# Weight casts in pieces of 1024 rows instead of 2048, three of them gated on the layer norm's progress

## The reference

```
xn  = layernorm(x)
s   = causal GQA attention(xn)           # 16 query heads, 4 kv heads, RoPE, then @ Wp.T
Wg  = (gate_w - 128) * gate_scale        # int32 [8192, 2048]; Wu likewise, Wd [2048, 8192]
h   = silu(xn @ Wg.T) * (xn @ Wu.T)
out = x + s * silu(h @ Wd.T)
```

## Time and profile before

| | us |
|---|---|
| median of 2 runs | 5322.83 |
| the two runs | 5040.26 and 5605.40 |
| the profiled execution | 5042.12 |
| its span, first to last instruction, on its slowest core (core 0) | 5039.6 |
| spans of the other seven cores | 4996.3 to 5036.2 |
| TensorE busy | 3874.6 (77% of the span) |
| VectorE, ScalarE, GpSimd busy | 984.7, 699.8, 165.9 |

### The profile page before, as it was taken

The page is one execution under the profiler, slowest core; times in us unless marked ns, Lnnn a source line. Parts: engine busy times, 40 slices in busy tenths (PEclk is TensorE's granted clock), DMA queues, the critical chain, the costliest instruction groups (busy, mean ns, idle before and its releaser), DMA issues.

```text
span 5039.6 us, 50095 instructions; the slowest of 8 cores (4996.3 to 5039.6 us)
## 1 busy us (share of the span) xinstructions
PE 3874.6 (77%) x16768; PEld 1651.2 (33%) x16768; DVE 984.7 (20%) x995; ACT 699.8 (14%) x1076; POOL 165.9 (3%) x308
## 2 busy tenths in 40 slices
PE   0001999939994891999979979999988499948998
PEld 0000444414442340444434432222233144424443
DVE  1111000000000000000024975555511000000010
ACT  0001111101110110111100025555500000000000
POOL 0000000000000000000000000000000000000000
PEclk9999999969997995999989989999999799979999
DMA  9996544785469598544221212100000655564553
GB/s 157 134 145 163 135 118 117 106 135 144 116 110 126 149 115 135 147 116 123 80 55 38 72 42 52 42 14 14 1 25 34 188 111 112 113 199 92 122 114 96
DMA packets 757036, 517.29 MB, mean 103 GB/s; under 512 B 686208, under 2 KB 694416, under 8 KB 743616
## 3 DMA queue, kind: packets, MB, share of 16 engines
q1 hardware_dynamic: 717952, 297.96, 25.8%
q0 software_dynamic: 36544, 207.74, 22.5%
q10 hardware_dynamic: 2304, 8.39, 0.4%
HBM read 329.36 MB, written 197.13 MB: 104 GB/s over the span
## 4 chain that ended last, share of the span: by engine, by line
PE 65%; SPq 17%; DVE 7%; another core or an unknown queue 6%; issue 3%; DMA 2%; ACT 1%; DVEq 0%; POOL 0%; ACTq 0%; POOLq 0%
PE b_ps L57 18%; SPq L57 17%; PE g_ps L57 14%; PE u_ps L57 13%; PE c_ps L57 5%; PE d_ps L57 4%; PE s_ps L57 4%; PE kq_ps L57 4%; PE o_ps L57 3%; DVE rc L57 1%; DVE tmpB L57 1%; DVE tmpA L57 1%; DVE qst L57 1%; DVE lc L57 1%
## 5 line engine op out<-in xcount | busy, mean ns | idle before, releaser
L57 PE MATMUL g_ps<-xnT,gu 128*128 128x512 bf16 x4096 | 901.6, 381 | 540.2 <-DMA gu<-wg_s 477.6
L57 PE MATMUL u_ps<-xnT,gu 128*128 128x512 bf16 x4096 | 903.7, 382 | 247.7 <-DVE h L57 241.4
L57 PE MATMUL b_ps<-wdr,hT 128*128 128x512 bf16 x4096 | 903.1, 384 | 193.5 <-DMA wdr<-wd_s 144.2
L57 PEld LDWEIGHTS g_ps<-xnT,gu 128*128 128x128 bf16 x4096 | 402.2, 98 | 1029.3 <-issue 551.1
L57 PEld LDWEIGHTS u_ps<-xnT,gu 128*128 128x128 bf16 x4096 | 402.7, 98 | 739.0 <-issue 261.7
L57 PEld LDWEIGHTS b_ps<-wdr,hT 128*128 128x128 bf16 x4096 | 404.5, 99 | 692.1 <-issue 220.8
L57 DVE SCALAR_TENSOR_TENSOR h<-u_ps,us_col,sil 128x2048 bf16<-128x2048 f32 x64 | 150.4, 2351 | 2022.3 <-PE u_ps L57 1560.1
L57 ACT ACTIVATE E<-s_ps 128x512 bf16<-128x512 f32 (+3 forms) x576 | 303.1, 526 | 209.5 <-PE s_ps L57 192.2
L57 ACT ACTIVATE sil<-g_ps,gs_col 128x2048 bf16<-128x2048 f32 x64 | 125.9, 1966 | 1393.8 <-PE g_ps L57 1393.7
L57 PE MATMUL kq_ps<-xnT,wsl 128*128 128x512 bf16 x1280 | 281.4, 381 | 32.5 <-DMA wsl<-wk_s 28.6
L57 PE MATMUL d_ps<-E,ones_bf 128*128 128x512 bf16 x640 | 253.8, 397 | 55.1 <-DVE E L57 48.6
(11 more groups left out here) (48 smaller groups left out, 1026.4 us busy)
## 6 DMA issues: line engine op xcount, KB each, us to landing
dwi<-dw SPq DMA_DIRECT2D x64, 1024.0 KB, 5.8
wg_s<-gw POOLq DMA_DIRECT2D x4, 8192.0 KB, 94.4
wu_s<-uw POOLq DMA_DIRECT2D x4, 8192.0 KB, 173.3
wd_s<-dwb POOLq DMA_DIRECT2D x64, 512.0 KB, 6.4
h_scr<-h POOLq DMA_DIRECT2D x64, 512.0 KB, 4.1
hT<-h_scr SPq DMA_DIRECT2D x128, 256.0 KB, 9.2
x_r<-x SPq DMA_DIRECT2D x16, 1024.0 KB, 50.8
x<-x POOLq DMA_DIRECT2D x64, 256.0 KB, 6.1
```

The lines of the kernel that those rows point to most:

```text
L57: r = getattr(e, meth)(*args, **kw)
```

## The change

A cast piece becomes 1024 rows (two groups), so there are eight pieces instead of four. Piece 0 is issued at the start without a wait. Pieces 1, 2 and 3 are also at the start of POOL's program, each behind a wait until 4, 8 or 12 tiles of the layer norm have been reduced. Pieces 4, 5, 6 and 7 are issued at groups 2, 4, 6 and 8. The slab fills wait for the piece that holds their rows.

```diff
-    def emit_gu_cast(qq):
-        r0 = qq * 2048
-        GQ("dma_start", wg_s[r0:r0 + 2048, :], gw_d[r0:r0 + 2048, :],
-           i=(f"stgu{qq}", 16))
-        GQ("dma_start", wu_s[r0:r0 + 2048, :], uw_d[r0:r0 + 2048, :],
-           i=(f"stgu{qq}", 16))
+    def emit_gu_cast(ch, w=()):
+        r0 = ch * 1024
+        GQ("dma_start", wg_s[r0:r0 + 1024, :], gw_d[r0:r0 + 1024, :],
+           w=w, i=(f"stgu{ch}", 16))
+        GQ("dma_start", wu_s[r0:r0 + 1024, :], uw_d[r0:r0 + 1024, :],
+           i=(f"stgu{ch}", 16))
 
     emit_gu_cast(0)
-    emit_gu_cast(1)
+    for ch in range(1, 4):
+        emit_gu_cast(ch, w=[("a_c1", min(4 * ch, 14))])
...
-                w.append((f"stgu{sg // 4}", 32))
+                w.append((f"stgu{sg // 2}", 32))
...
-            if sg == 4:
-                emit_gu_cast(2)
-            if sg == 8:
-                emit_gu_cast(3)
+            if sg in (2, 4, 6, 8):
+                emit_gu_cast(4 + (sg - 2) // 2)
```

## The result

The changed kernel is faster: the ratio to the kernel before is **0.9749**, with a 95% interval of 0.972 to 0.9778. Its profiled execution took 4912.42 us, against 5042.12 before: 129.7 us less, where 106.6 were forecast. It is luck, and no more, that the median of all 11 runs of the changed kernel, 4936.27, equals the forecast: it is pulled up, as the 5322.83 shown before was, by executions in which one half of the cores runs slower, and five of the eleven took 4909 to 4914.

A forecast was written before the change was run, and what follows sets the result against it. TensorE was taken to stand still behind casts, pieces 2 and 3 costing 187.8 us together. Four stalls of 20.3 us, 81 in all, replace them: 5042.1 - 106.6 + 0 for the start = 4936 us, range 4890 to 4985.

The forecast's parts named there:

- The mechanism: In the loop: a stall of 13 to 27 us in each of four places, the start unchanged; chance 0.74.
- tail C: Time from a loop cast's end to TensorE's start: 39.7 us at piece 2, 45.3 at piece 3; 44.2 forecast.
- room: In the loop, the time between a slab fill's start and the step that needs it: 119.5 us.
- The length of a half cast: Loop cast with half the rows, from issue to landing: 80 us taken, between 77.3 and 83.9.
- the due times: When TensorE's loop steps start without a stall, at 27.63 us a step; `g_ps` of step 20 at 1040.5.
- The first block behind a gap: TensorE's first block after a loop stall: 16.29 us instead of 13.98, so 2.3 us more a place.
- the 1.7 us: Growth of tail C: 1.3 transposes left over after half a cast, at 1.3 us each.
- The start: Gated casts beside the layer norm: 0 us change, with -10 and +10 for the two ends.
- The sum: Whole kernel: -106.6 us from the loop stalls and 0 from the start, giving 4936 us.
- the rival in which it runs into them: At the start, piece 3 runs beside SP's transposes and delays `xnT`, at most 80 us: 5016; chance 0.10.
- The stall that goes wholly: In the loop: if C fell by 18 us, no stall would be left, 4854 us; chance 0.07.
- The stall that costs the same whatever the cast: In the loop: each of four places costs 93.9 us whatever the cast's size, 5230 us; chance 0.04.

The follow-up runs named there:

- one_place: The changed kernel with all four loop pieces issued at group 4, as one cast; ratio 1.0106 to the kernel before, 5107 us at best.
- two_places: The changed kernel with its loop casts put back in pairs at groups 4 and 8, gates kept; ratio 0.9969 to the kernel before.
- the experiment: The changed kernel with the three gates at the start taken away, all four start pieces queued at once; ratio 0.9747 to the kernel before.
- dwi_between: The changed kernel with one load of `dwi` moved on SP to between the two slab fills; ratio 0.9569 to the kernel before.
- attn_spread: The changed kernel with the ten attention casts issued two at each of groups 9 to 13 instead of all at group 10; ratio 0.9512.
- all_hidden: The changed kernel with casts after the first 1024 rows in 512-row loop pieces, `dwi` load between fills, attention casts singly at groups 4 to 13; 4634.98 us.
- spread_final: As spread_light, but the piece of group 2 waits for the first block of `u_ps` instead of `g_ps`; ratio 0.8995 to the kernel before.
- spread_light: As all_hidden, with group 2's piece gated on the first `g_ps` block and the four `wp` casts moved behind the attention stage's first block; ratio 0.9061.

## Why the prediction was right or wrong

*The mechanism: right.* Four gaps in front of `g_ps` of steps 12, 20, 28 and 36, ended by silu, none in front of `u_ps`; the store of `h` no longer a cause there. The arithmetic of the stall (start of the cast + its length + tail C - room) holds from 42 to 309 us of cast: nothing at 42, 61 / 4 = 15 at 80, 92 at 158, 246 at 309.

*The length of a half cast: right.* 80 us taken, 79.0 to 81.0 measured. So were the due times. The first block behind a gap cost 1.5 to 2.6 us, where 2.3 were taken.

*The tail C: the step that failed, in its size.* The prediction had C = 44.2, "in the mean" 42.5 of two cases and 1.7 for transposes left over. Measured: 39.4 as the mean of four. The 4.8 us come four times, 19 us, nearly the whole difference between 81 and 61. Two errors are in it. The 45.3 of piece 3 was a case and not a level: the tails in one_place and two_places were 36 to 42 again. The trace of the kernel before had the answer on its other cores: its 16 tails, read in the same way, lie between 37.1 and 45.3, and their mean is 39.4 too, so the tail didn't grow at all. And the 1.7 us were read from a window that began too early. The q1 row starts at 935, when the cast was issued but not yet moving. Two windows of the kernel before, 935 to 940 and 940 to 1090 us, show it (packets, MB, share):

```profile
q1 hardware_dynamic: 585, 0.14, 13.3%
```
```profile
q0 software_dynamic: 590, 16.52, 97.2%
q1 hardware_dynamic: 591, 0.15, 0.7%
```

Nearly half of the 1342 pieces passed in the first five. So 1.2 transposes pass beside a whole cast, and beside half a cast of the changed kernel, in the window from 947 to 1023 us, it is 0.9:

```profile
q0 software_dynamic: 446, 8.91, 97.3%
q1 hardware_dynamic: 437, 0.10, 1.1%
```

Half a cast leaves 0.3 of a transpose over, not 1.3. The two rows of each window also say how the queues share the engines: one packet of each in turn, 590 to 591 and 446 to 437, whatever is in it. A packet of the cast holds 28 KB in the mean of the first window, one of the transposes 250 bytes. In the layer norm of the kernel before, from 139 to 184 us, three queues pass 129, 130 and 129 packets; there a packet of q1 holds 7 KB of `x`, and 45 us is what a tile of 128 rows takes beside the casts. The Trainium skill's rule, in "DMA: Bandwidth & Descriptors", section "Queues, rings and completion order", is that a whole packet of typically 9 to 17 descriptors goes from one queue in its turn. The trace agrees with the turns by packet, and not with that size: the 128 bf16 columns of one row of a transpose are 256 bytes, so a turn of q1 carried a single piece.

*The start: within its bounds.* 0 with 10 us either way was said, and -8.4 came, of which the gates give about 5 by the experiment. The gaps opened where they were worked out, but half as wide: on core 3 pieces 1 and 2 landed at 196.6 and 292.1, and the gates behind them passed at 201.4 and 296.7, 5 us each instead of 9. The last piece was over before the transposes began; the rival in which it runs into them did not occur.

*The sum.* -106.6 forecast, -129.7 measured: 20 us of the difference are the four stalls and 8 the start, less the 6 lost behind the loop. That is outside neither the bounds of the loop (-80 to -135) nor the stated range, but both terms erred to the same side, and it left "faster by over 2%" at 0.52 where 2.5% came out.

*The rivals.* The stall that goes wholly needed a C of 26 us; dwi_between, which takes the 20 us of the up slab's issues out of it, is this case, and it took a change of SP's order. The stall that costs the same whatever the cast is refuted by one_place.

## What to carry to other kernels

A bulk transfer issued from one queue costs what it overruns of the slack of the transfers behind it; so cut it into pieces no longer than that slack, and issue one for each period of the loop. Follow the wait through the queues to its end: TensorE waited here for a silu, behind a dequantisation, behind a load, behind a fill, and moving that one load removed the stall at all four places of 80 us. It didn't at the long attention casts, where a second wait, for a store in the cast's own queue, was as long. When a bulk transfer is gated, gate it on the landing or the use of what it must not delay, and not on the event just before: a release 16 us earlier (271.4 against 287.6) took back 36 us of gain.

## What was not expected of the hardware

- Beside a cast in rows of 16384 elements, the transposing DMAs of the other queue come almost to a stop: 0.7% to 1.1% of the DMA time, about one transpose in 150 us, where alone they take 1.3 us each. The queues pass packet for packet (590 to 591), so what a queue gets beside a cast goes by the size of its pieces: 0.15 MB in 150 us in pieces of 250 bytes, but 0.94 MB in 45 us for the 7 KB pieces of `x` in the layer norm.
- The tail behind a cast hardly depends on the length of the cast: 36 to 43 us, once 45, behind casts of 80, 156 and 309 us.
- Even at 84% of DMA time over 560 us (attn_spread, core 3) TensorE can run without a gap, if the load is even. At 86 to 89% short gaps came back on some cores (all_hidden, spread_final), and the share alone doesn't tell which: from 500 to 2000 us core 2 of spread_light lost nothing at 87%.
